# One Hydra mixer on one core: x times silu(z) formed ahead of the fd bank, and four orders of work rewritten

## The chip, the core and the metric

One core of one Trainium2 chip runs the whole program. The metric is the device time of one execution in microseconds. The profile is one execution, recorded by the hardware profiler; its times count from the first instruction. PE is TensorE, DVE is VectorE, ACT is ScalarE, POOL is GpSimd, SP is SyncE, which issues the DMAs.

## The reference

Two transformer-like blocks with AdaLN modulation over 1024 tokens of 512 features. Block 0 is attention and a routed MLP, block 1 a Hydra mixer and a gated MLP with LoRA. The change is in block 1's mixer, of which the kernel computes this part twice (y = 0, 1) for each half (hf) of 512 tokens:

```python
h = gelu(x @ w_down.T + b_down)
z, xBC = split(h @ in_w.T)
xs = silu(conv(xBC))                                  # sequence length 1: one tap
y  = xs * repeat(xs @ fcD_w.T + D, 64, axis=-1)       # the scans are shifted out at length 1
yz = y * silu(z)
h  = (yz * rsqrt(mean(yz ** 2) + 1e-5) * norm_w) @ out_w.T
# after the second pass:
h  = xmid + alpha * xmid + (1 - alpha) * h
x  = x_init + (h @ w_up.T + b_up)                     # then layernorm, modulation, MLP
```

## The kernel before

Features lie on the 128 partitions, tokens along the free axis, in two halves `tok[0]` and `tok[1]`. A half of a 256-feature tensor is two tiles (m = 0, 1) of 128x512 float32. TensorE writes into eight PSUM banks that are handed out in turn by a planner (`Banks`), whose order is that of the list `MIXER`; `filled` waits until TensorE has filled a bank, `evacuated` until its reader is done.

Each engine runs the mixer by a list of its own, written out by hand: `MIXER` (TensorE), `MIXER_ACT`, `MIXER_DVE`, `MIXER_POOL`. An engine works strictly in the order of its list. An entry is (step, y, hf):

- `mid`, `in`, `fd`: TensorE projects down, makes the xs and z banks (four matmuls), and from xs the two fd banks (four matmuls). ScalarE turns the first into xs and sz = silu(z).
- VectorE's `fd`, for each m: yz = (bank + D) * xs (line 2028), then yz = yz * sz (line 2032). `fd_first` and `fd_second` are m = 0 and m = 1.
- `out`: TensorE multiplies yz by Who (two matmuls) and sums squares, which ScalarE makes from yz (16 small matmuls); ScalarE copies the result to hor and the mean square to hms; GpSimd takes the inverse root (line 2364).
- `dg`: VectorE spreads the root into a diagonal tile (line 2041), both inputs in SBUF. `scale`: TensorE broadcasts it into the bank rbc (one matmul), VectorE multiplies it by hor into hof (2048, or 2053 for y = 1, there followed by 2055, which adds midf). hof feeds `in` of the next y, or `up`.
- `up`: TensorE makes two banks of 128x512; VectorE adds them to x (line 1894) and takes layernorm statistics (1652, 1658 to 1664) of what it has added.
- Beside this chain: `rows` prepares row vectors; `centred` (2001, eight tiles in all) writes rt; GpSimd's `shift` (2342) adds a row to x; `rest` (2007) adds rt times the deviation to x and must be done before `up`; `merge` (1996) adds LoRA to the next weights, ScalarE's and GpSimd's `w13` (1530, 2347) split them in two.

Behind the mixer GpSimd's root gives the last layernorm's scale, ScalarE normalises tiles 0 and 1 and VectorE tiles 2 and 3 (2074), TensorE transposes them (884), and VectorE, ScalarE and GpSimd split the transposed halves for the MLP (1691, 1695, 1355, 2174).

A step by VectorE or GpSimd that TensorE needs is signalled by a semaphore; SP's queue waits for freed weight slots (`piece_done`) and for `r_ready` before its next loads.

Of the kernel before, what the change touches and what calls it, by code (L numbers as in the profile page):

```python
# [23 lines left out]
ALU = mybir.AluOpType  # L24
# [7 lines left out]
KC = D // P  # L32
# [52 lines left out]
class Banks:  # L85
# [27 lines left out]
    def get(self, name, turn=0):  # L113
# [4 lines left out]

MIXER = [("mid", 0, 0), ("in", 0, 0), ("fd", 0, 0), ("ln", 0, 1), ("mid", 0, 1), ("out", 0, 0), ("in", 0, 1),
         ("scale", 0, 0), ("fd", 0, 1), ("in", 1, 0), ("out", 0, 1), ("fd", 1, 0), ("scale", 0, 1), ("in", 1, 1),  # L120
         ("lora", 0, 0), ("out", 1, 0), ("fd", 1, 1), ("scale", 1, 0), ("out", 1, 1), ("up", 0, 0), ("scale", 1, 1),
         ("up", 0, 1), ("up", 1, 0), ("up", 1, 1)]
MIXER_ACT = [("mid", 0, 0), ("in", 0, 0), ("ln", 0, 1), ("fd", 0, 0), ("mid", 0, 1), ("out", 0, 0), ("in", 0, 1),
             ("fd", 0, 1), ("in", 1, 0), ("out", 0, 1), ("fd", 1, 0), ("in", 1, 1), ("out", 1, 0), ("w13", 0, 0),
             ("fd", 1, 1), ("out", 1, 1)]
MIXER_DVE = [("fd", 0, 0), ("rows", 0, 0), ("dg", 0, 0), ("scale", 0, 0), ("fd", 0, 1), ("centred", 0, 0),
             ("centred", 0, 1), ("dg", 0, 1), ("fd_first", 1, 0), ("scale", 0, 1), ("fd_second", 1, 0), ("rest", 0, 0), ("merge", 0, 0),
             ("rest", 0, 1), ("dg", 1, 0), ("fd", 1, 1), ("scale", 1, 0), ("dg", 1, 1), ("up", 0, 0), ("scale", 1, 1),
             ("up", 0, 1), ("up", 1, 0), ("up", 1, 1)]
MIXER_POOL = [("out", 0, 0), ("wup", 0, 0), ("out", 0, 1), ("shift", 0, 0), ("shift", 0, 1), ("out", 1, 0),  # L130
              ("out", 1, 1), ("w13", 1, 1)]
FD_PARTS = {"fd": (0, 1), "fd_first": (0,), "fd_second": (1,)}
SPLIT_LNS = (1, 3)

# [263 lines left out]
def adaln_two_blocks(nc, a, out):  # L398
    banks, pieces, prods = plan()
    with ExitStack() as ctx:  # L400
# [12 lines left out]
        def sem(name):  # L413
            return ctx.enter_context(nc.semaphore(name))
# [4 lines left out]
        def ar(word, *dims):  # L419
# [183 lines left out]
        ab_in, ab_ready, rn_ready, xb_ready, r_ready = (  # L603
            sem("mixer_rows_loaded"), sem("mixer_rows_ready"), sem("mixer_rest_centred"),
            sem("mixer_rest_shifted"), sem("mixer_rest_ready"))
        yz_ready, sq_ready, ho_ready = sem("yz_ready"), sem("yz_squared"), sem("hydra_out_ready")
        eps_ready, hor_ready = sem("eps_ready"), sem("hydra_out_copied")
        ms_ready, mr_ready, dg_ready = sem("mean_squares_ready"), sem("inverse_rms_ready"), sem("inverse_rms_diagonal_ready")
# [1035 lines left out]
        def _(dve):  # L1644
            V = nc.vector
# [364 lines left out]
            for kind, y, hf in MIXER_DVE:  # L2010
# [11 lines left out]
                elif kind in FD_PARTS:  # L2022
                    for m in FD_PARTS[kind]:
                        n = 4 * y + 2 * hf + m
                        b = filled(dve, ("fd", y, hf, m))
                        if y:
                            dve.wait_ge(sq_ready, n - 3)
                        V.scalar_tensor_tensor(out=yz[:, m, tok[hf]], in0=ps[:, b, :], scalar=cols[:, C_D + m:C_D + m + 1],
                                               in1=xs[:, m, tok[hf]], op0=ALU.add, op1=ALU.mult).then_inc(read_b[b], 1)
                        evacuated(dve, ("z", y, hf, m))  # L2030
                        evacuated(dve, ("fd", y, hf, m))
                        V.tensor_tensor(yz[:, m, tok[hf]], yz[:, m, tok[hf]], sz[:, m, tok[hf]], ALU.mult)\
                            .then_inc(yz_ready, 1)
                elif kind == "rest":
                    for t in range(4 * hf, 4 * hf + 4):
                        rest(t)
# [20 lines left out]
                elif kind == "merge":  # L2057
                    for c in range(2):
                        merge(("w13", c), [("lora", "F", c), ("lora3", "F", c)])
                elif kind == "up":  # L2060
                    for t in (4 * y + 2 * hf, 4 * y + 2 * hf + 1):
                        add_x(("wup", t), t, x[:, t, :])
                        if t % 4:
                            evacuated(dve, ("wup", t - 1))
                            ln_stat(y, t % 4 - 1)
                    if hf:
                        evacuated(dve, ("wup", t))
                        ln_stat(y, 3)
                        ln_finish(3, y)
                    if (y, hf) == (1, 0):  # L2070
                        dve.wait_ge(ln_nb, 1)
                        filled(dve, ("ln", 2, 1, KC - 1))
                        for t in range(2, 4):
                            V.tensor_scalar(xnb[:, t, :], x[:, t, :], rs[:, 0, t:t + 1], nb[:, 0, t:t + 1], ALU.mult,
                                            ALU.add).then_inc(ln_xn, 1)
            ln_full(3, 0)
            ln_full(3, 1)

# [49 lines left out]
        def _(pool):  # L2128
# [230 lines left out]
            for kind, y, hf in MIXER_POOL:  # L2359
# [3 lines left out]
                        pool.wait_ge(dg_ready, 2 * y + hf)  # L2363
                    nc.gpsimd.tensor_tensor(hrs[:, :], hms[:, :], mh[:, :], ALU.pow).then_inc(mr_ready, 1)
                elif kind == "shift":
                    pool.wait_ge(dg_ready, 2)
                    for t in range(4 * hf, 4 * hf + 4):
                        rest(t)
                elif kind == "wup":
                    raw_loaded(pool, "wup")  # L2370
                    pool.wait_ge(rows_ready, 1)
                    nc.gpsimd.tensor_tensor(Wuo[:, :], raw[:, piece_slot("wup"), 0:D], t36[:, :], ALU.mult)\
                        .then_inc(piece_done, 1)
                elif kind == "w13":
                    pool.wait_ge(yz_ready, 4 * y + 2 * hf + 2)
                    for k in range(2):
                        w13_lo(k, ("w13", k), k)
            rstd(3, 0)
# [115 lines left out]
```

## Time and profile before

| | |
|---|---|
| median of 3 runs | 757.67 us (755.9 to 758.73) |
| span of the profiled execution | 756.9 us |
| TensorE matmul busy | 713.5 us, 94% |
| VectorE busy | 474.8 us, 63% |
| ScalarE busy | 318.3 us, 42% |
| GpSimd busy | 314.5 us, 42% |
| the mixer on TensorE | 482.64 to 556.28 us |

The profile names each instruction by engine, line, operation and tiles (output, arrow, inputs). A matmul of float32 is recorded as two instructions, so x8 are four matmuls. The square bracket at the end of a line is the time that the engine sat idle ahead of it and what ended that. A timeline row merges like neighbours: its start, and the time from the first start to the last end.

### The profile page before, as it was taken

Reading aid. Unit: us, or ns where it says so; the run is one execution under the profiler, and the core shown is the slowest. Engines: PE = TensorE matmul, PEld = TensorE weight load, DVE = VectorE, ACT = ScalarE, POOL = GpSimd, SP = SyncE. Lnnn points to the kernel's source line nnn. Section 1 sums busy time; section 2 is a strip of 40 time slices with the busy share of each in tenths; the row PEclk is TensorE's granted clock in tenths of the full one; section 3 lists DMA queues with packets and bytes.
Section 4 is the critical chain, followed back from the end, with each engine's and each line's share of the span. In section 5 each row is a group of like instructions: output and inputs, shape, how many; then the busy total and the mean of one; then the engine's idle time right before and its main releaser. Section 6 shows DMA issues by size and latency. Waiting matters only on the chain.

```text
span 756.9 us, 10266 instructions
## 1 busy us (share of the span) xinstructions
PE 713.5 (94%) x3718; PEld 431.1 (57%) x3718; DVE 474.8 (63%) x716; ACT 318.3 (42%) x536; POOL 314.5 (42%) x254
## 2 busy tenths in 40 slices
PE   4998899999999999889999999999789999999998
PEld 2444334333333332258788888554358788877886
DVE  3787677888888885237765558768895433338211
ACT  3311267677767767751335310554234223223100
POOL 0325673756565574861456233115431222125300
PEclk9999799999999999999999999999889999999999
DMA  8357516263251200230023100213010111111111
GB/s 307 107 126 220 124 43 164 73 123 54 72 123 26 30 3 29 75 113 14 29 62 105 56 1 0 78 50 66 1 68 1 57 55 39 44 55 57 42 69 42
DMA packets 24111, 53.00 MB, mean 70 GB/s; under 512 B 4252, under 2 KB 8100, under 8 KB 23044
## 3 DMA queue, kind: packets, MB, share of 16 engines
q1 hardware_dynamic: 24068, 52.44, 25.0%
q8 instruction: 26, 0.43, 0.2%
q14 instruction: 17, 0.14, 0.1%
HBM read 45.63 MB, written 6.60 MB: 69 GB/s over the span
## 4 chain that ended last, share of the span: by engine, by line
PE 76%; DVE 12%; issue 5%; DMA 2%; ACT 2%; SPq 2%; POOL 1%; DVEq 0%; ACTq 0%; POOLq 0%
PE ps L867 73%; DVE mxp L1810 2%; DMA rq<-in_mask 1%; DVE st L1652 1%; PE ps L884 1%; DVE xnb L1676 1%; ACT pr L1456 1%; DVE x L2007 1%; PE ps L1051 1%; DVE rt L1691 1%; DVE x L1894 1%; PE ps L1119 0%; DVE dg L2041 0%; SPq L717 0%; DVE qsw L1861 0%
## 5 line engine op out<-in xcount | busy, mean ns | idle before, releaser
L867 PE MATMUL ps<-arena 128*128 128x512 f32 (+1 forms) x1404 | 325.9, 392 | 1.4 <-DVE arena L1695 0.7
L867 PEld LDWEIGHTS ps<-arena 128*128 128x128 f32 (+1 forms) x1404 | 259.6, 186 | 59.3 <-DVE arena L1695 1.4
L1810 DVE TENSOR_REDUCE mxp<-ps 128x2 f32<-128x1024 f32 (+3 forms) x160 | 172.8, 1115 | 44.5 <-PE ps L867 43.9
L1456 ACT ACTIVATE pr<-ps 128x512 f32<-128x512 f32 x288 | 162.1, 596 | 75.7 <-PE ps L867 71.9
L867 PE MATMUL ps<-Qst,Kst 99*128 99x512 bf16 x288 | 100.2, 389 | 6.1 <-ACT pr L1456 4.8
L867 PE MATMUL ps<-Kst,Qst 96*128 96x512 bf16 (+3 forms) x384 | 98.6, 334 | 5.4 <-DVE mxp L1810 4.2
L2248 POOL TENSOR_TENSOR pr<-pr,cap 128x512 int32<-128x512 int32 x56 | 71.1, 1285 | 38.3 <-ACT pr L1456 38.3
L867 PE MATMUL ps<-pr,vr 128*32 128x512 f32 x576 | 76.5, 604 | 0.0
L867 PEld LDWEIGHTS ps<-Qst,Kst 99*128 99x128 bf16 x288 | 24.5, 98 | 79.7 <-ACT pr L1456 63.9
L867 PEld LDWEIGHTS ps<-Kst,Qst 96*128 96x128 bf16 x384 | 36.4, 99 | 51.3 <-DVE mxp L1810 20.2
L2347 POOL TENSOR_TENSOR arena<-raw,arena 128x1024 fp32r<-128x1024 f32 x11 | 26.7, 2431 | 80.2 <-ACT arena L1530 80.2
L867 PE MATMUL ps<-maskb,identb 128*128 128x128 bf16 (+1 forms) x264 | 53.1, 229 | 0.0
L2088 DVE TENSOR_TENSOR xnb<-ps,full 128x512 f32<-128x512 f32 x22 | 15.2, 691 | 49.0 <-PE ps L867 46.0
L1894 DVE TENSOR_TENSOR x<-ps,x 128x512 f32<-128x512 f32 x24 | 16.2, 685 | 46.2 <-PE ps L867 46.2
L1605 ACT ACTIVATE arena<-xnb 128x512 f32 (+1 forms) x22 | 13.9, 632 | 45.9 <-DVE xnb L2088 45.9
L2164 POOL TENSOR_TENSOR rs<-ve,mh 128x4 f32<-128x4 f32 x8 | 8.1, 1016 | 57.2 <-DVE ve L1664 57.1
L867 PEld LDWEIGHTS ps<-maskb,identb 128*128 128x128 bf16 x264 | 26.3, 100 | 8.5 <-issue 2.9
L867 PE MATMUL ps<-h0T,wq 128*128 128x512 f32 x64 | 30.0, 600 | 0.5 <-ACT wq L1389 0.5
L2090 DVE TENSOR_TENSOR arena<-xnb,arena 128x512 f32 (+1 forms) x22 | 15.3, 697 | 20.0 <-ACT arena L1605 20.0
L867 PEld LDWEIGHTS ps<-pr,vr 128*32 128x32 f32 x576 | 11.5, 108 | 24.0 <-issue 21.4
L1519 ACT ACTIVATE full<-ps,s 128x512 f32<-128x512 f32 x8 | 5.5, 689 | 45.9 <-PE ps L867 45.9
L2238 POOL TENSOR_TENSOR wsum<-wsum,wmr 128x640 f32<-128x640 f32 (+2 forms) x18 | 23.7, 1315 | 1.5
(203 smaller groups left out, 822.2 us busy)
## 6 DMA issues: line engine op xcount, KB each, us to landing
wmr<-in_wmr SPq DMA_DIRECT2D x8, 1280.0 KB, 11.0
raw<-in_w SPq DMA_DIRECT2D x16, 512.0 KB, 3.3
Qst<-q_parts SPq DMA_DIRECT2D x42, 128.0 KB
q_parts<-qparts SPq DMA_DIRECT2D x3, 768.0 KB, 5.0
x<-in_x SPq DMA_DIRECT2D x8, 256.0 KB, 6.0
wm<-in_wm SPq DMA_DIRECT2D x4, 512.0 KB, 7.5
raw<-in_up SPq DMA_DIRECT2D x8, 256.0 KB, 2.6
raw<-in_down SPq DMA_DIRECT2D x8, 256.0 KB, 2.6
```

What stands on the lines that cost most here:

```text
L867: return nc.tensor.matmul(outp, lhs, rhs, start=start, stop=stop, skip_group_check=True)
L884: last = nc.tensor.transpose(ps[:, b, t * P:(t + 1) * P], xnb[:, t, c * P:(c + 1) * P], ident[:, :])
L1456: A(pr[:, k % PRING, :], ps[:, 4 + k % 2, :], ACT.Exp, scale=float(DH) ** -0.5).then_inc(exp_done, 1)
L1605: A(gT[0][:, bass.ds(c, 1), tok[hf]].rearrange("p o n -> p (o n)"), xnb[:, s, :], ACT.Copy)\
L1810: V.tensor_reduce(mxp[:, kh, g0:g0 + heads, i].rearrange("p (b e) -> p b e", e=per), units, AXX, ALU.max)\
L1894: V.tensor_tensor(x[:, t, :], ps[:, b, :], other, ALU.add).then_inc(read_b[b], 1)
L2088: V.tensor_tensor(xnb[:, s, :], ps[:, b, :], full[:, s, :], ALU.mult).then_inc(read_b[b], 1)
L2090: V.tensor_tensor(gT[1][:, bass.ds(c, 1), tok[hf]].rearrange("p o n -> p (o n)"), xnb[:, s, :], gT[0][:, bass.ds(c, 1), tok[hf]].rearrange ...
L2164: root = nc.gpsimd.tensor_tensor(rs[:, hf, :], ve[:, hf, :], mh[:, :], ALU.pow)
L2238: ins = nc.gpsimd.tensor_tensor(wsum[:, n0:n1], wsum[:, n0:n1], to, ALU.add)
L2248: nc.gpsimd.tensor_tensor(v, v, cap[:, :].unsqueeze(1).to_broadcast([P, G, P]), ALU.mult).then_inc(masked, 1)
L2347: nc.gpsimd.tensor_tensor(W13[slot][1].rearrange("p a b c -> p (a b c)"), raw[:, piece_slot(name), :], W13[slot][0].rearrange("p a b c -> ...
```

## The change

VectorE gets a step `gate` that forms yz = xs * sz as soon as both are there, and its fd step becomes one pass, yz = (bank + D) * yz, after which it frees the bank. A new semaphore `xz_ready` goes between the two. The tiles 2 and 3 of the last normalisation become a step of their own, `norm`. The lists are rewritten: TensorE's `up(0,1)` goes ahead of `scale(1,1)`; VectorE's and GpSimd's lists as shown; GpSimd's shifts of half hf now wait for the diagonal of that half, and its `w13` waits for a diagonal in place of yz and stands ahead of the last root.

```diff
--- before.py
+++ after.py
@@ -118,17 +118,18 @@
 
 MIXER = [("mid", 0, 0), ("in", 0, 0), ("fd", 0, 0), ("ln", 0, 1), ("mid", 0, 1), ("out", 0, 0), ("in", 0, 1),
          ("scale", 0, 0), ("fd", 0, 1), ("in", 1, 0), ("out", 0, 1), ("fd", 1, 0), ("scale", 0, 1), ("in", 1, 1),
-         ("lora", 0, 0), ("out", 1, 0), ("fd", 1, 1), ("scale", 1, 0), ("out", 1, 1), ("up", 0, 0), ("scale", 1, 1),
-         ("up", 0, 1), ("up", 1, 0), ("up", 1, 1)]
+         ("lora", 0, 0), ("out", 1, 0), ("fd", 1, 1), ("scale", 1, 0), ("out", 1, 1), ("up", 0, 0), ("up", 0, 1),
+         ("scale", 1, 1), ("up", 1, 0), ("up", 1, 1)]
 MIXER_ACT = [("mid", 0, 0), ("in", 0, 0), ("ln", 0, 1), ("fd", 0, 0), ("mid", 0, 1), ("out", 0, 0), ("in", 0, 1),
              ("fd", 0, 1), ("in", 1, 0), ("out", 0, 1), ("fd", 1, 0), ("in", 1, 1), ("out", 1, 0), ("w13", 0, 0),
              ("fd", 1, 1), ("out", 1, 1)]
-MIXER_DVE = [("fd", 0, 0), ("rows", 0, 0), ("dg", 0, 0), ("scale", 0, 0), ("fd", 0, 1), ("centred", 0, 0),
-             ("centred", 0, 1), ("dg", 0, 1), ("fd_first", 1, 0), ("scale", 0, 1), ("fd_second", 1, 0), ("rest", 0, 0), ("merge", 0, 0),
-             ("rest", 0, 1), ("dg", 1, 0), ("fd", 1, 1), ("scale", 1, 0), ("dg", 1, 1), ("up", 0, 0), ("scale", 1, 1),
-             ("up", 0, 1), ("up", 1, 0), ("up", 1, 1)]
-MIXER_POOL = [("out", 0, 0), ("wup", 0, 0), ("out", 0, 1), ("shift", 0, 0), ("shift", 0, 1), ("out", 1, 0),
-              ("out", 1, 1), ("w13", 1, 1)]
+MIXER_DVE = [("gate", 0, 0), ("fd", 0, 0), ("rows", 0, 0), ("centred", 0, 0), ("dg", 0, 0), ("scale", 0, 0),
+             ("gate", 0, 1), ("fd", 0, 1), ("centred", 0, 1), ("rest", 0, 0), ("gate", 1, 0), ("dg", 0, 1),
+             ("fd_first", 1, 0), ("scale", 0, 1), ("fd_second", 1, 0), ("rest", 0, 1), ("merge", 0, 0),
+             ("gate", 1, 1), ("dg", 1, 0), ("fd", 1, 1), ("scale", 1, 0), ("up", 0, 0), ("dg", 1, 1),
+             ("up", 0, 1), ("scale", 1, 1), ("norm", 0, 0), ("up", 1, 0), ("up", 1, 1)]
+MIXER_POOL = [("out", 0, 0), ("wup", 0, 0), ("shift", 0, 0), ("out", 0, 1), ("shift", 0, 1), ("out", 1, 0),
+              ("w13", 1, 0), ("out", 1, 1)]
 FD_PARTS = {"fd": (0, 1), "fd_first": (0,), "fd_second": (1,)}
 SPLIT_LNS = (1, 3)
 
@@ -603,6 +604,7 @@
         ab_in, ab_ready, rn_ready, xb_ready, r_ready = (
             sem("mixer_rows_loaded"), sem("mixer_rows_ready"), sem("mixer_rest_centred"),
             sem("mixer_rest_shifted"), sem("mixer_rest_ready"))
+        xz_ready = sem("xs_times_gate_ready")
         yz_ready, sq_ready, ho_ready = sem("yz_ready"), sem("yz_squared"), sem("hydra_out_ready")
         eps_ready, hor_ready = sem("eps_ready"), sem("hydra_out_copied")
         ms_ready, mr_ready, dg_ready = sem("mean_squares_ready"), sem("inverse_rms_ready"), sem("inverse_rms_diagonal_ready")
@@ -2023,14 +2025,22 @@
                     for m in FD_PARTS[kind]:
                         n = 4 * y + 2 * hf + m
                         b = filled(dve, ("fd", y, hf, m))
+                        dve.wait_ge(xz_ready, n + 1)
+                        V.scalar_tensor_tensor(out=yz[:, m, tok[hf]], in0=ps[:, b, :], scalar=cols[:, C_D + m:C_D + m + 1],
+                                               in1=yz[:, m, tok[hf]], op0=ALU.add, op1=ALU.mult).then_inc(yz_ready, 1)
+                        dve.wait_ge(yz_ready, n + 1)
+                        nc.vector.sem_inc(read_b[b], 1)
+                elif kind == "gate":
+
+                    if y:
+                        filled(dve, ("hout", 0, hf))
+                    for m in range(2):
+                        evacuated(dve, ("xs", y, hf, m))
+                        evacuated(dve, ("z", y, hf, m))
                         if y:
-                            dve.wait_ge(sq_ready, n - 3)
-                        V.scalar_tensor_tensor(out=yz[:, m, tok[hf]], in0=ps[:, b, :], scalar=cols[:, C_D + m:C_D + m + 1],
-                                               in1=xs[:, m, tok[hf]], op0=ALU.add, op1=ALU.mult).then_inc(read_b[b], 1)
-                        evacuated(dve, ("z", y, hf, m))
-                        evacuated(dve, ("fd", y, hf, m))
-                        V.tensor_tensor(yz[:, m, tok[hf]], yz[:, m, tok[hf]], sz[:, m, tok[hf]], ALU.mult)\
-                            .then_inc(yz_ready, 1)
+                            dve.wait_ge(sq_ready, 2 * hf + m + 1)
+                        V.tensor_tensor(yz[:, m, tok[hf]], xs[:, m, tok[hf]], sz[:, m, tok[hf]], ALU.mult)\
+                            .then_inc(xz_ready, 1)
                 elif kind == "rest":
                     for t in range(4 * hf, 4 * hf + 4):
                         rest(t)
@@ -2067,12 +2077,12 @@
                         evacuated(dve, ("wup", t))
                         ln_stat(y, 3)
                         ln_finish(3, y)
-                    if (y, hf) == (1, 0):
-                        dve.wait_ge(ln_nb, 1)
-                        filled(dve, ("ln", 2, 1, KC - 1))
-                        for t in range(2, 4):
-                            V.tensor_scalar(xnb[:, t, :], x[:, t, :], rs[:, 0, t:t + 1], nb[:, 0, t:t + 1], ALU.mult,
-                                            ALU.add).then_inc(ln_xn, 1)
+                elif kind == "norm":
+                    dve.wait_ge(ln_nb, 1)
+                    filled(dve, ("ln", 2, 1, KC - 1))
+                    for t in range(2, 4):
+                        V.tensor_scalar(xnb[:, t, :], x[:, t, :], rs[:, 0, t:t + 1], nb[:, 0, t:t + 1], ALU.mult,
+                                        ALU.add).then_inc(ln_xn, 1)
             ln_full(3, 0)
             ln_full(3, 1)
 
@@ -2363,7 +2373,7 @@
                         pool.wait_ge(dg_ready, 2 * y + hf)
                     nc.gpsimd.tensor_tensor(hrs[:, :], hms[:, :], mh[:, :], ALU.pow).then_inc(mr_ready, 1)
                 elif kind == "shift":
-                    pool.wait_ge(dg_ready, 2)
+                    pool.wait_ge(dg_ready, hf + 1)
                     for t in range(4 * hf, 4 * hf + 4):
                         rest(t)
                 elif kind == "wup":
@@ -2372,7 +2382,7 @@
                     nc.gpsimd.tensor_tensor(Wuo[:, :], raw[:, piece_slot("wup"), 0:D], t36[:, :], ALU.mult)\
                         .then_inc(piece_done, 1)
                 elif kind == "w13":
-                    pool.wait_ge(yz_ready, 4 * y + 2 * hf + 2)
+                    pool.wait_ge(dg_ready, 2 * y + hf + 1)
                     for k in range(2):
                         w13_lo(k, ("w13", k), k)
             rstd(3, 0)
```

## Rows read from the trace of the kernel before

**Rows 1.** The page: busy time, share of span and instructions of each engine

```profile
PE 713.5 (94%) x3718; PEld 431.1 (57%) x3718; DVE 474.8 (63%) x716; ACT 318.3 (42%) x536; POOL 314.5 (42%) x254
```

**Rows 2.** TensorE's timeline through the mixer: start, us, line, operation, tiles

```profile
511.36 3.60 PE L867 MATMUL ps<-hof,Whi 128*128 128x512 f32 x8
514.79 1.88 PE L867 MATMUL ps<-yz,Who 128*128 128x512 f32 x4
...
521.73 1.02 PE L867 MATMUL ps<-dg,ones 128*128 128x512 f32 x2
523.60 3.70 PE L867 MATMUL ps<-hof,Whi 128*128 128x512 f32 x8 [0.85 <-DVE hof L2048]
...
531.51 3.68 PE L867 MATMUL ps<-xs,Wfd 128*128 128x512 f32 x8
537.73 1.75 PE L867 MATMUL ps<-dg,ones 128*128 128x512 f32 x2 [2.54 <-DVE dg L2041]
...
543.88 1.96 PE L867 MATMUL ps<-Wuo,hof 128*128 128x512 f32 x4
548.32 2.08 PE L867 MATMUL ps<-dg,ones 128*128 128x512 f32 x2 [2.48 <-DVE dg L2041]
550.18 6.10 PE L867 MATMUL ps<-Wuo,hof 128*128 128x512 f32 x12
558.90 3.45 PE L884 MATMUL ps<-ident,xnb 128*128 128x128 f32 x16 [2.62 <-ACT xnb L1592]
...
566.91 2.02 PE L867 MATMUL ps<-arena 128*128 128x512 f32 x7 [0.66 <-DVE arena L1695]
```

**Rows 3.** Table by stretches: busy time of each engine, granted clock, DMA

```profile
537.70:541.70 4.00, 3.97 (x5) 1.42 (x6) 3.76 (x6) 1.26 (x2) 0.00 (x0) 0.57 0.00 0
...
548.30:552.00 3.70, 3.68 (x5) 1.69 (x6) 3.21 (x5) 0.00 (x0) 2.17 (x1) 0.54 0.77 235
```

**Rows 4.** VectorE's timeline through the mixer

```profile
505.12 1.74 DVE L2041 TENSOR_TENSOR dg<-ident,hrs 128x512 f32<-128x512 f32 x1 [2.94 <-POOL hrs L2364]
...
513.02 5.38 DVE L2001 SCALAR_TENSOR_TENSOR rt<-x,mv,Abc 128x512 f32<-128x512 f32 x8
519.77 0.69 DVE L2041 TENSOR_TENSOR dg<-ident,hrs 128x512 f32<-128x512 f32 x1 [1.36 <-POOL hrs L2364]
...
531.95 2.47 DVE L1996 SCALAR_TENSOR_TENSOR raw<-ps,raw 128x512 f32<-128x512 f32 x4
534.35 2.72 DVE L2007 SCALAR_TENSOR_TENSOR x<-rt,rs,x 128x512 f32<-128x512 f32 x4
536.99 0.68 DVE L2041 TENSOR_TENSOR dg<-ident,hrs 128x512 f32<-128x512 f32 x1
...
545.44 2.82 DVE L2041 TENSOR_TENSOR dg<-ident,hrs 128x512 f32<-128x512 f32 x1 [3.46 <-POOL hrs L2364]
...
558.53 0.68 DVE L1894 TENSOR_TENSOR x<-ps,x 128x512 f32<-128x512 f32 x1
...
562.25 0.17 DVE L1664 TENSOR_SCALAR ve<-mv 128x4 f32<-128x4 f32 x1
562.33 2.97 DVE L1691 TENSOR_SCALAR rt<-ps,modc 128x512 f32<-128x512 f32 x4
```

**Rows 5.** GpSimd's timeline through the mixer

```profile
520.54 12.62 POOL L2342 TENSOR_TENSOR x<-x,Bbc 128x512 f32<-128x512 f32 x8 [0.81 <-DVE dg L2041]
...
544.39 1.01 POOL L2364 TENSOR_TENSOR hrs<-hms,mh 128x4 f32<-128x4 f32 x1 [10.27 <-ACT hms L1579]
545.37 5.10 POOL L2347 TENSOR_TENSOR arena<-raw,arena 128x1024 fp32r<-128x1024 f32 x2
```

**Rows 6.** Groups of VectorE's passes by line; last, durations of line 2007, min/median/max

```profile
L2032 DVE TENSOR_TENSOR yz<-yz,sz 128x512 f32<-128x512 f32 x8 | 6.0, 748 | 0.8
L2028 DVE SCALAR_TENSOR_TENSOR yz<-ps,cols,xs 128x512 f32<-128x512 f32 x8 | 6.0, 746 | 1.3 <-PE ps L867 1.1 <-DVE hof L2048 0.2
...
L2007 DVE SCALAR_TENSOR_TENSOR x<-rt,rs,x x8: 735/1244/1764, 525.2 to 536.3; 128x512 f32<-128x512 f32 x8
```

## The prediction

> **What bounds the kernel now.** I read the page's busy times first: TensorE is busy 94% of the span [rows 1], so the kernel can only gain where TensorE waits or runs slowly. TensorE's timeline through the mixer is next [rows 2]. Up to 535.2 us it hardly pauses: the largest hole, 0.85 us, is ahead of 523.60. Then three holes come in a row: 2.54 us ahead of 537.73, 2.48 us ahead of 548.32 and 2.62 us ahead of 558.90; a smaller one (0.66 us) ahead of 566.91. The granted clock falls from full (2.4 GHz) to half (1.2 GHz) behind each large hole [rows 3]: a float32 matmul of 128x512 takes 0.86 us at full clock (3.43 for the four from 511.36 to 514.79), so the seven from 548.32 to 556.28 should take 6.2 us with their tail and take 7.96, a loss of 1.8 us; the transposes at 558.90 take 3.45 us and should take about 2. Together: 8.3 us of holes and about 5 us of slow clock. Everything behind 567 us is TensorE's own work and moves with it.
>
> VectorE's timeline says why [rows 4]. Ahead of 537.73 TensorE wants the diagonal dg(1,0); VectorE begins it at 536.99, after the merges and four residual passes (rest) that end at 537.07, though GpSimd's root had come at 534.1 (behind eight shifts that end at 533.16 [rows 5]). Ahead of 548.32 it wants dg(1,1): its root is done at 545.40, but the pass takes 2.82 us instead of 0.68, because GpSimd starts its w13 subtraction at 545.37 [rows 5]. Ahead of 558.90 it wants normalised x, which needs VectorE's sums of up(0,1), queued behind scale(1,1).
>
> **Price of contention.** A VectorE pass whose two inputs are both in SBUF is stretched by a GpSimd pass: a rest takes 0.74 us alone and up to 1.76 beside the shifts (+1.03), dg +2.14 beside the longer w13 pass [rows 4 to 6]. The fd pass that reads PSUM takes 0.74 to 0.75 in all eight places, two of them during the shifts [rows 6]. So the new fd pass (PSUM and yz) is immune, and the new gate passes (xs, sz) are exposed: 0.69 each alone, 1.7 (a shift) to 2.8 (a w13 pass) blocked.
>
> The Trainium skill's page "SBUF — State Buffer", section "Who interferes with whom", says that a VectorE instruction with two SBUF inputs and a GpSimd instruction that reads SBUF exclude each other for the whole instruction. The trace agrees (0.68 against 2.82 us); it speaks against moving more two-input passes among the shifts, and feeds the last rival.
>
> **The change, part by part.**
>
> 1. *Gate formed early.* Per half, four passes (0.74 + 0.69, twice) behind the fd bank become two (0.74 each) behind it and two gates before. VectorE's sum stays: 2.9 us. Behind the second bank's fill the path shrinks from 1.55 to 0.75 us. For halves (0,0), (0,1), (1,0) TensorE asks for yz later than it was ready even before, so that is worth nothing; it counts in (1,1).
>
> 2. *Half (0,1) and the first shifts.* centred(0,0) (4 x 0.67 = 2.7 us) goes into the 2.94 us in which VectorE idled before dg at 505.12 [rows 4]: free. shift(0,0) now starts when dg(0,0) is done, 506.9, and runs beside gate(0,1), which starts about 508.9 (506.9, TensorE's broadcast 1.3, the hof pass 0.7). With two blockings the gates end at 512.1, the fd passes at 513.7, before out(0,1) at 514.79: hidden with 1.1 us over. Then VectorE has centred(0,1) 2.7, rest(0,0) 2.7 and gate(1,0) 1.4: it reaches dg(0,1) at 520.4, not 519.77. TensorE needs that dg at 521.73 [rows 2], so 0.6 us of cover is left and 523.60 stays. Bounds: nothing, to 2.5 us late (four shift passes can block four passes, 4.1 us; two are in my value, and 0.6 is covered, so 1.5, plus a blocking of up to 1.0 by the 1.01 us root).
>
> 3. *Half (1,0) into (1,1), the first large hole.* VectorE is free at 524.5. shift(0,1) has begun at about 521.0 and ends near 527; rest(0,1) is done near 528.9 (two blocked), merges 2.47 us to 531.4, gate(1,1) to 532.8. GpSimd's root no longer waits for shifts: its input comes 0.5 us behind the issue of TensorE's next step (543.88 and 544.39 [rows 2, 5]; here 531.51), at 532.0, root 533.0, dg(1,0) to 533.7. TensorE's fd(1,1) issues until 534.95, so the hole is gone. fd(1,1)'s last pass runs 535.1 to 535.8, and out(1,1) issues at 535.8. The w13 subtractions now wait for dg(1,0), 533.7 to 538.8, and beside them scale(1,0)'s second pass (midf and hof, both in SBUF, due at 536.7) is blocked by up to 2.1 us: 539.4 against 539.2 when TensorE wants it. up(0,0) starts at about 539.45 instead of 543.88: **4.4 us** gained, 2.5 of hole, the rest clock. Bounds: if every rest is blocked (4 x 1.7) and both gates, dg(1,0) ends near 536.6: the gain shrinks to 1.1.
>
> 4. *Half (1,1), the second hole.* The root comes 0.5 us behind up(0,0)'s issue as before [rows 2, 5], ending at 540.75 with GpSimd free from 538.8. But dg(1,1) is now queued on VectorE behind up(0,0): add, add, sums. The second bank fills at 541.3, so these end at 542.5 and dg(1,1) at 543.2, without the 2.1 us of contention. up(0,1) covers TensorE until 542.9: a hole of 0.3 us. scale(1,1) issues at 543.2 and fills at 544.2. On VectorE it now stands behind up(0,1), whose two adds, three statistics and small passes take 3.9 us (the same set runs from 558.53 to 562.42 [rows 4]): 543.1 to 547.0, then hof's two passes to 548.4. Only then can up(1,0) go. So 2.48 us of hole become **4.2 us** at another place, and the clock falls there again (1.8 us lost on the four matmuls): up(1,1) fills at 553.8 against 556.4. Of 4.4 us, 1.8 are given back here. Bounds: 1.4 to 3.5 us lost to the clock.
>
> 5. *Third hole.* up(0,1)'s statistics are done at 547.0, the root at 548.3, ScalarE's and VectorE's normalised tiles by 550.0: before up(1,1) ends, so the transposes follow it at once at 553.8 (558.90 before) at full clock. "norm" standing ahead of up(1,0) on VectorE costs nothing: it ends at 549.4 and the first bank fills at 550.3. What is late next is VectorE's tail: up(1,1)'s set starts at 553.25 (bank and queue), 3.9 us, then 4.45 us from 562.42 to the release at about 566.87 [rows 2, 4]: 553.25 + 3.9 + 4.45 = 561.6. TensorE waits there about 1.4 us where it waited 0.66.
>
> **Sum.** 566.9 − 561.6 = 5.3 us. Cross-check by holes and clock: 8.3 + 5.3 before; 0.3 + 4.2 + about 2.0 (of it 0.6 on ScalarE's halves) + 1.8 after, which is 5.3 less. The profiled execution spans 756.9 us and the median of the runs is 757.67, 0.7 above it; 756.9 − 5.3 = 751.6 for a span, **752.4** for a median. Loads for w13 start when slots are freed, now about 9 us earlier; the swap of up(0,1) and scale(1,1) only exchanges banks that are read long before.
>
> **Rivals.**
> - *Better cover.* The clock does not fall behind the 4.2 us hole, or is full again by the time matmuls resume: 1.8 less, 750.6. Against it: each of three holes above 2.4 us was followed by half clock [rows 2, 3]. Chance 0.10.
> - *Given back.* The clock falls also behind the last wait (1.4 us, between the 0.85 that left it full and the 2.48 that did not), 1.7 us, and dg(1,0) or the hof combine comes up to 1.5 us late: 754.1 to 755.9, taken as 755. Chance 0.24.
> - *It does not do what it says.* VectorE's queue is still at rest and merge at 535 to 536, so dg(1,0) moves by 1 us only, and the long hole of part 4 eats that: 757. For it: VectorE's queue has no pause from 531.95 to 537.67 [rows 4]. Against: four rests (2.7 us) left that stretch. Chance 0.06.
> - *Slower: two-input passes blocked in series.* From the moment merge ends after about 533.8, ScalarE's w13 copies run to 536, the w13 subtractions to 541, and VectorE's hof combine and dg stand in them: 2.1 us twice. With 1.5 us lost in part 2, 3.3 in part 3 (4.4 to 1.1), and the clock lost at the end (1.7): 752.4 + 4.2 + 1.5 + 3.3 + 1.7 = 763 at worst; three quarters of it, 760, is taken. It decides once 5.3 us of it, half, fall in the path. The rule quoted above from the Trainium skill's page "SBUF — State Buffer" is the same mechanism. Chance 0.08.
>
> **How the numbers follow.** Forecast 0.52 (751 to 753.9). This kernel's measurement can tell about 0.5% (3.8 us) from no change, so faster means below 753.9: 0.52 + 0.10 + 0.02 of the given-back case = 0.64. Same: 0.22 + 0.06 = 0.28. Slower: 0.08. Range 749.6 to 756.8: it takes in the better case and its own spread, the given-back case, and leaves out about 0.04 below and 0.12 above.
>
> **What would show it.** Right: TensorE without a hole before scale(1,0); dg(1,1) at 0.7 us; a hole of about 4 us before up(1,0), with half clock behind it; transposes directly behind up(1,1). Wrong: gate(0,1) or rest blocked so often that TensorE waits ahead of in(1,1) or scale(1,0) by over 1 us; dg above 1 us; half clock after TensorE's wait for VectorE's halves.

## The result and the profile after

The changed kernel takes 753.56 us (median of 7 runs, 751.74 to 754.48) beside 756.89 for the kernel before in the same runs. The ratio is 0.9944, with a 95% interval of 0.9928 to 0.996: by the ratio 4.2 us faster (0.56%), by the two medians 3.3. The forecast was 752.4, the range 749.6 to 756.8.

The profiled execution of the changed kernel took 754.48 us and spans 752.7; before it spanned 756.9. TensorE is busy for 1.8 us less, as the page's first row shows (engines, busy us, share of the span), which answers to [rows 1]:

```profile
PE 711.7 (95%) x3718; PEld 429.2 (57%) x3718; DVE 472.8 (63%) x716; ACT 318.0 (42%) x536; POOL 314.6 (42%) x254
```

So of the 4.2 us some 2.4 are waiting, and 1.8 are the same 3718 matmul records in less time: over the mixer stretch that is measured below, the granted clock averages 0.91 of full before and 0.94 after. TensorE's timeline of the changed kernel, beside [rows 2]:

```profile
507.89 3.60 PE L869 MATMUL ps<-xs,Wfd 128*128 128x512 f32 x8
...
523.67 3.70 PE L869 MATMUL ps<-hof,Whi 128*128 128x512 f32 x8 [0.86 <-DVE hof L2058]
...
531.58 3.68 PE L869 MATMUL ps<-xs,Wfd 128*128 128x512 f32 x8
535.10 1.02 PE L869 MATMUL ps<-dg,ones 128*128 128x512 f32 x2
...
539.58 3.67 PE L869 MATMUL ps<-Wuo,hof 128*128 128x512 f32 x8
543.51 1.12 PE L869 MATMUL ps<-dg,ones 128*128 128x512 f32 x2 [0.26 <-DVE dg L2051]
548.78 6.54 PE L869 MATMUL ps<-Wuo,hof 128*128 128x512 f32 x8 [4.14 <-issue]
555.16 1.91 PE L886 MATMUL ps<-ident,xnb 128*128 128x128 f32 x16
...
562.63 2.03 PE L869 MATMUL ps<-arena 128*128 128x512 f32 x7 [1.16 <-DVE arena L1697]
```

The hole of 2.54 us ahead of scale(1,0) is gone (535.10 follows fd(1,1) at once), and up(0,0) starts at 539.58 instead of 543.88. The hole ahead of scale(1,1) is 0.26 us instead of 2.48. A new one of 4.14 us stands ahead of up(1,0), at 548.78; its bracket says `issue`, which names no releaser, and VectorE's second pass into hof, which up(1,0) reads, ends just before, at 548.68. The four matmuls behind it, eight records, take 6.54 us; at full clock the four of up(0,0) and up(0,1) take 3.67. The transposes follow without a hole. The last wait is 1.16 us instead of 0.66. The clock column of the table by stretches (seventh figure behind the times, as in [rows 3]) shows the half clock behind the new hole:

```profile
544.60:548.80 4.20, 0.06 (x2) 0.05 (x1) 3.97 (x13) 0.03 (x1) 1.32 (x2) 0.87 0.00 0
548.80:555.20 6.40, 6.40 (x9) 2.62 (x10) 3.88 (x7) 1.49 (x2) 0.00 (x0) 0.55 0.00 0
```

VectorE's timeline, beside [rows 4]: the two gates of half (0,1) among the shifts, dg(0,1), the combine of scale(1,0), dg(1,1), and the two hof passes of scale(1,1).

```profile
509.09 2.58 DVE L2042 TENSOR_TENSOR yz<-xs,sz 128x512 f32<-128x512 f32 x2 [0.23 <-DVE hof L2058]
...
520.95 0.69 DVE L2051 TENSOR_TENSOR dg<-ident,hrs 128x512 f32<-128x512 f32 x1 [0.91 <-POOL hrs L2374]
...
537.02 2.46 DVE L2065 SCALAR_TENSOR_TENSOR hof<-midf,alf,hof 128x512 f32<-128x512 f32 x1
...
542.78 0.68 DVE L2051 TENSOR_TENSOR dg<-ident,hrs 128x512 f32<-128x512 f32 x1
...
547.20 0.69 DVE L2063 TENSOR_TENSOR hof<-ps,hor 128x512 f32<-128x512 f32 x1
547.93 0.75 DVE L2065 SCALAR_TENSOR_TENSOR hof<-midf,alf,hof 128x512 f32<-128x512 f32 x1
```

dg(1,1) takes 0.68 us, not 2.82. The combine, 0.75 us alone, takes 2.46 beside the w13 subtractions, and the two gates 2.58, not 1.28. GpSimd's timeline, beside [rows 5]: the root of half (0,1), and the two w13 subtractions.

```profile
518.70 2.22 POOL L2374 TENSOR_TENSOR hrs<-hms,mh 128x4 f32<-128x4 f32 x1 [5.90 <-ACT hms L1581]
...
534.26 4.67 POOL L2357 TENSOR_TENSOR arena<-raw,arena 128x1024 fp32r<-128x1024 f32 x2 [0.81 <-DVE dg L2051]
```

The root takes 2.22 us instead of 1.01: gate(1,0) runs on VectorE meanwhile. dg(0,1) ends at 521.64, and TensorE's scale(0,1) issues at 521.69, so the cover of 0.6 us that the prediction counted had shrunk to nothing.

**A measure for the experiments.** Whole times scatter by about 0.5% for one kernel, so each profile is also read over one stretch: from the first matmul of fd(0,1) to the release of the first MLP wait (the start of the x7 group). The kernel before begins its stretch with this row:

```profile
507.92 3.60 PE L867 MATMUL ps<-xs,Wfd 128*128 128x512 f32 x8
```

It is 566.91 − 507.92 = **58.99 us** before and 562.63 − 507.89 = **54.74 us** after, 4.25 us less: the whole difference of the spans (4.2) lies in it. What comes behind the stretch takes 190.0 to 190.1 us in every profile but e9's; what comes ahead of it varies by up to 6 us (503.51 in e6 to 509.44 in e5), though no edit touches it.

A stretch is one execution. The same kernel gave 54.74 and 54.22 us (e11), and the difference comes from the clock behind the new hole: up(1,0) starts 40.89 and 40.90 us into it. So for differences below 0.5 us I read where up(1,0) starts. The ratios, of 4 to 10 runs each, don't bear out every size. Put over the span of 756.9 us, the stretches of e1 (0.990), e4 (0.991), e3 and e6 (1.002) and e7 (1.003) lie outside the intervals of their own whole times in the table. What an edit does to the order of work is read from the stretch; how much it gives on average is not.

### The profile page after: what moved, and what is told of

The parts are those of the page before. It is cut to its first block, busy times and chain, and to the rows that moved or that the text cites. A ratio compares the mean times of both kernels' runs of the same rounds, so it can differ in the third digit from the quotient of the medians.

```text
span 752.7 us, 10280 instructions
## 1 busy us (share of the span) xinstructions
PE 711.7 (95%) x3718; PEld 429.2 (57%) x3718; DVE 472.8 (63%) x716; ACT 318.0 (42%) x536; POOL 314.6 (42%) x254
## 4 chain that ended last, share of the span: by engine, by line
PE 79%; DVE 10%; issue 4%; DMA 2%; ACT 2%; SPq 2%; POOL 1%; DVEq 0%; ACTq 0%; POOLq 0%
PE ps L869 76%; DVE mxp L1812 2%; DMA rq<-in_mask 1%; PE ps L886 1%; DVE st L1654 1%; DVE xnb L1678 1%; ACT pr L1458 1%; PE ps L1053 1%; DVE rt L1693 1%; PE ps L1121 0%; SPq L719 0%; DVE x L1896 0%; DVE qsw L1863 0%; DMA q_parts<-parts 0%; POOL arena L2357 0%
## 5 line engine op out<-in xcount | busy, mean ns | idle before, releaser
L1896 DVE TENSOR_TENSOR x<-ps,x 128x512 f32<-128x512 f32 x24 | 16.4, 687 | 50.2 <-PE ps L869 50.2
L2343 POOL TENSOR_TENSOR yrs<-yve,mh 128x1 f32<-128x1 f32 x8 | 6.0, 755 | 43.9 <-DVE yve L1974 43.9
```

The source lines that it names most:

```text
L1896: V.tensor_tensor(x[:, t, :], ps[:, b, :], other, ALU.add).then_inc(read_b[b], 1)
```

## The experiments

| kernel | stretch, us | ratio to before (95%) |
|---|---|---|
| before | 58.99 | |
| changed | 54.74 | 0.9944 (0.9928 to 0.996) |
| e11, changed again | 54.22 | 0.9934 (0.991 to 0.9957) |
| e1, tail as before | 51.68 | 0.993 (0.9906 to 0.9953) |
| e2, w13 behind the root | 55.06 | 0.9949 (0.9929 to 0.9969) |
| e3, no gate | 60.67 | 1.0 (0.9981 to 1.0018) |
| e4, hole filled | 52.39 | 0.9943 (0.992 to 0.9965) |
| e5, no gate, w13 behind | 55.17 | 0.9956 (0.9942 to 0.997) |
| e6, shifts as before | 60.16 | 0.9988 (0.9973 to 1.0003) |
| e7, gate alone on before | 61.30 | 0.9988 (0.9972 to 1.0004) |
| e8, e1 with norm on ScalarE | 53.04 | 0.9906 (0.9882 to 0.993) |
| e9, VectorE's tail alone | 53.27 | 0.9931 (0.9914 to 0.9949) |
| e10, e1 with its hole filled | 51.86 | 0.992 (0.9894 to 0.9945) |

**1. Which order took the first hole away.** e6 keeps gate, w13 and tail, and puts the residual work back on both engines (... stands for what is left out):

```diff
-             ... ("centred", 0, 0), ("dg", 0, 0), ..., ("centred", 0, 1), ("rest", 0, 0), ("gate", 1, 0), ("dg", 0, 1), ...,
-             ("rest", 0, 1), ("merge", 0, 0), ("gate", 1, 1), ("dg", 1, 0), ...
+             ... ("dg", 0, 0), ..., ("centred", 0, 0), ("centred", 0, 1), ("gate", 1, 0), ("dg", 0, 1), ...,
+             ("rest", 0, 0), ("merge", 0, 0), ("rest", 0, 1), ("gate", 1, 1), ("dg", 1, 0), ...
-             ... ("wup", 0, 0), ("shift", 0, 0), ("out", 0, 1), ("shift", 0, 1), ...      # MIXER_POOL
+             ... ("wup", 0, 0), ("out", 0, 1), ("shift", 0, 0), ("shift", 0, 1), ...
-                    pool.wait_ge(dg_ready, hf + 1)      # each shift
+                    pool.wait_ge(dg_ready, 2)
```

> The changed kernel, gates, w13 and tail included, with centred, rest and merge on VectorE and the shifts on GpSimd in the order of the kernel before, both shifts behind the second diagonal. Theory (the early shifts and rests made the hole ahead of scale(1,0) go): dg(1,0) runs at about 538 on the clock of the kernel before, a hole of 3 to 4 us and half clock are back; same stretch 59 to 61 us, 4 to 6 more than the changed kernel. Rival (another part removed that hole): within 1 us of 54.74.

The stretch is 60.16 us, 5.4 more than in the changed kernel. TensorE's timeline of e6, scale(1,0) and up(0,0), has the hole again, and behind it a wait of 0.83 us. The row names w13, but that had ended at 538.43; the combine on VectorE, the last row here, takes 2.71 us beside w13 (late too now) and ends at 538.97:

```profile
533.72 1.13 PE L869 MATMUL ps<-dg,ones 128*128 128x512 f32 x2 [2.95 <-DVE dg L2051]
...
539.07 5.20 PE L869 MATMUL ps<-Wuo,hof 128*128 128x512 f32 x8 [0.83 <-POOL arena L2357]
```

```profile
536.26 2.71 DVE L2065 SCALAR_TENSOR_TENSOR hof<-midf,alf,hof 128x512 f32<-128x512 f32 x1
```

The theory holds, and the size is as forecast. The whole times agree: the interval of e6 (0.9973 to 1.0003) lies above that of the changed kernel. Moving the residual work forward is what makes the first hole go; VectorE's order and GpSimd's were moved back together, so their shares aren't known.

**2. What the gate is worth.** e7 puts it alone into the kernel before, e3 takes it out of the changed one, e5 takes it out and moves w13 back too, e2 moves only w13 back. e3 and e5 pass over the step `gate` and use the fd step of the kernel before:

```diff
-  V.scalar_tensor_tensor(out=yz[...], in0=ps[:, b, :], ..., in1=yz[...], ...)
+  V.scalar_tensor_tensor(out=yz[...], in0=ps[:, b, :], ..., in1=xs[...], ...)
+  V.tensor_tensor(yz[...], yz[...], sz[...], ALU.mult)
```

e2 and e5 change GpSimd's list:

```diff
-              ("w13", 1, 0), ("out", 1, 1)]
+              ("out", 1, 1), ("w13", 1, 1)]
-                    pool.wait_ge(dg_ready, 2 * y + hf + 1)
+                    pool.wait_ge(yz_ready, 4 * y + 2 * hf + 2)
```

> The changed kernel's orders with the fd step of the kernel before: no gate, two passes behind each bank. Theory (the orders make the gain, the gate takes next to nothing off the path): out(1,1)'s second matmul waits about 0.2 us, the hof pass ahead of in(1,1) starts 0.1 to 0.3 us later; 0.2 to 0.6 us more than the changed kernel, ratio to before about 0.995. Rival (the gate carries the gain, 0.8 us at each half that is on the path): 1.6 to 3 us more, ratio 0.996 to 0.998.

> The changed kernel with GpSimd's two w13 subtractions back behind the last root, waiting for yz as before. Theory (the move is worth what dg(1,1) lost to contention, 2.1 us, less what the hof combine of (1,0) loses now): the combine takes 0.75 us instead of 2.46, up(0,0) starts 0.2 us earlier, dg(1,1), now at 542.78, falls into the subtractions (540.9 to 546) and takes 1.1 to 2.8 us; 0.3 to 2 us more than the changed kernel, ratio to before 0.995 to 0.997. Rival (with dg queued behind up(0,0), the move no longer matters): within 0.3 us of the changed kernel.

> The kernel without the gate (e3_two_pass_fd) and with GpSimd's w13 subtractions back behind the last root. Read from fd(0,1)'s first matmul to the release of the first MLP wait, which took 58.99 us before, 54.74 in the changed kernel and 60.67 without the gate. Theory (the gate's worth is only that no two-input pass of fd(1,1) meets the w13 subtractions): the passes of fd(1,1) take 0.7 each again, the loss of 5.9 us goes almost wholly, 55.3 us. Rival (the longer chain behind the fd bank costs by itself): 57 us or more.

> The kernel before with the gate and one-pass fd alone; all other steps in the order of the kernel before. Theory (alone it saves 0.8 us behind the last fd bank at best, where TensorE waits for dg and not for yz): stretch 58.0 to 59.5 us, ratio 0.998 to 1.001. Rival (the gate's own worth is the larger part of the gain): 56 us or less.

e3 refuted my theory, and its rival was too mild: the stretch is 60.67 us, 5.9 more, and the whole gain is gone (ratio 1.0, interval above that of the changed kernel). VectorE's timeline of e3 shows the second passes of fd(1,1), 0.69 us alone:

```profile
531.76 2.21 DVE L2034 TENSOR_TENSOR yz<-yz,sz 128x512 f32<-128x512 f32 x1
...
534.74 1.99 DVE L2034 TENSOR_TENSOR yz<-yz,sz 128x512 f32<-128x512 f32 x1
```

Both inputs are in SBUF, and both run beside the w13 subtractions (531.07 to 536.18), GpSimd's row:

```profile
531.07 5.11 POOL L2360 TENSOR_TENSOR arena<-raw,arena 128x1024 fp32r<-128x1024 f32 x2 [0.80 <-DVE dg L2054]
```

TensorE's timeline of e3, the two matmuls of out(1,1):

```profile
534.11 1.10 PE L869 MATMUL ps<-yz,Who 128*128 128x512 f32 x2 [0.84 <-DVE yz L2034]
536.78 2.07 PE L869 MATMUL ps<-yz,Who 128*128 128x512 f32 x2 [1.57 <-DVE yz L2034]
```

They wait 0.84 and 1.57 us, and the clock then drops. With w13 moved back as well (e5) the passes take 0.69 each and the stretch is 55.17 us: 0.1 more than e2 (55.06), which has the gate. TensorE's up(1,0) with (1,1), first of e2, then of e5:

```profile
548.33 6.52 PE L869 MATMUL ps<-Wuo,hof 128*128 128x512 f32 x8 [4.15 <-issue]
```

```profile
550.73 6.66 PE L869 MATMUL ps<-Wuo,hof 128*128 128x512 f32 x8 [4.14 <-issue]
```

Counted from the stretch's start (507.13 and 509.44) they begin at 41.20 and 41.29 us, so the 0.1 us is there ahead of the clock too. The long chain costs next to nothing by itself; 5.5 of the 5.9 us that e3 loses are the collision. VectorE's timeline of e2, the combine and dg(1,1):

```profile
536.25 0.75 DVE L2065 SCALAR_TENSOR_TENSOR hof<-midf,alf,hof 128x512 f32<-128x512 f32 x1
...
541.82 1.19 DVE L2051 TENSOR_TENSOR dg<-ident,hrs 128x512 f32<-128x512 f32 x1
```

The combine is clean (0.75 for 2.46), dg is stretched by half a microsecond (1.19 for 0.68), and the balance is 0.32 us, the bottom of the range that the theory gave and the top of the rival's: the two can't be told apart. dg(1,1), queued behind up(0,0), meets only the end of the first subtraction. Gate and early w13 together are thus worth 55.17 − 54.74 = 0.4 us in these profiles (41.29 − 40.89 at up(1,0)). The ratios (0.9944, 0.9949, 0.9956) can't tell the three kernels apart.

e7's time is that of the kernel before within its interval, which the theory said, but its stretch is 61.30, outside. TensorE's timeline of e7, scale(1,0), out(1,1) and up(0,0):

```profile
534.01 1.13 PE L868 MATMUL ps<-dg,ones 128*128 128x512 f32 x2 [1.74 <-DVE dg L2050]
535.96 3.75 PE L868 MATMUL ps<-yz,Who 128*128 128x512 f32 x4 [0.83 <-DVE yz L2028]
...
542.78 3.76 PE L868 MATMUL ps<-Wuo,hof 128*128 128x512 f32 x4
```

The hole is shorter (1.74 us), yet the second wait behind it (0.83) and a half clock that lasts from 535 to 552 us lose more than that. The gate of (1,1) stands between dg(1,0) and fd(1,1) there, where it hides nothing and is itself what out(1,1) waits for. The size isn't typical: this execution's mean clock, 0.984, is the lowest of the ten (the others 0.989 to 0.995), and their ratio (0.9972 to 1.0004) has no room for 2.3 us more. That the gate alone brings nothing, both show.

**3. The new hole.** e1 puts the end of both lists back:

```diff
 MIXER:     - ("up", 0, 0), ("up", 0, 1), ("scale", 1, 1), ("up", 1, 0)
            + ("up", 0, 0), ("scale", 1, 1), ("up", 0, 1), ("up", 1, 0)
 MIXER_DVE: - ("up", 0, 0), ("dg", 1, 1), ("up", 0, 1), ("scale", 1, 1), ("norm", 0, 0), ("up", 1, 0), ("up", 1, 1)
            + ("dg", 1, 1), ("up", 0, 0), ("scale", 1, 1), ("up", 0, 1), ("up", 1, 0), ("norm", 0, 0), ("up", 1, 1)
```

> The changed kernel with the end of TensorE's and VectorE's lists in the order of the kernel before: scale(1,1) ahead of up(0,1) on TensorE; on VectorE dg(1,1) ahead of up(0,0), scale(1,1) ahead of up(0,1), norm behind up(1,0). Theory (the new tail costs: dg and scale(1,1) wait in VectorE's queue behind up, which opens the 4.14 us hole): root at 540.9, dg to 541.6, scale(1,1) on VectorE behind up(0,0) to about 544.8, up(1,0) on TensorE at about 545 instead of 548.78 with hardly a hole; a hole of about 3 us comes back ahead of the transposes, at about 551.5 instead of 555.16; the first MLP wait ends near 559.2 instead of 562.63: 3.4 us less than the changed kernel, ratio to before about 0.990. Rival (the new tail pays, since it removes the hole ahead of the transposes): 2 us more than the changed kernel, ratio about 0.997.

Its TensorE timeline, from scale(1,1) to the first MLP wait:

```profile
538.52 1.12 PE L869 MATMUL ps<-dg,ones 128*128 128x512 f32 x2 [0.15 <-DVE dg L2051]
...
541.74 3.67 PE L869 MATMUL ps<-Wuo,hof 128*128 128x512 f32 x8 [0.38 <-issue]
548.42 2.66 PE L886 MATMUL ps<-ident,xnb 128*128 128x128 f32 x16 [3.01 <-ACT xnb L1594]
...
556.42 2.03 PE L869 MATMUL ps<-arena 128*128 128x512 f32 x7 [0.52 <-DVE arena L1697]
```

up(1,0) has 0.38 us of hole instead of 4.14 and starts 37.0 us into the stretch instead of 40.9. A hole of 3.01 us is back ahead of the transposes, and still the stretch is 51.68 us, 3.06 less than in the changed kernel (3.4 forecast). The ratio doesn't tell the two apart (0.993, from 4 runs). e9 changes VectorE's order alone, from up(0,1) on:

```diff
-             ("up", 0, 1), ("scale", 1, 1), ("norm", 0, 0), ("up", 1, 0), ("up", 1, 1)]
+             ("scale", 1, 1), ("up", 0, 1), ("up", 1, 0), ("norm", 0, 0), ("up", 1, 1)]
```

> The changed kernel with only VectorE's last steps in another order: scale(1,1) ahead of up(0,1), norm behind up(1,0); TensorE's order and dg(1,1) behind up(0,0) stay. The stretch is again from fd(0,1)'s first matmul to the release of the first MLP wait (54.74 us in the changed kernel, 51.68 in e1_tail_as_before). Theory (of the hole of 4.14 us, the larger part is scale(1,1) standing behind up(0,1) on VectorE): the hole shrinks to 1.5 us, the clock stays full, VectorE's last statistics end 2.2 us earlier, stretch 52.5 us. Rival (dg(1,1) behind up(0,0) and TensorE's swap are what costs): 54 us or more.

```profile
543.35 3.67 PE L869 MATMUL ps<-Wuo,hof 128*128 128x512 f32 x8 [1.68 <-issue]
550.03 1.97 PE L886 MATMUL ps<-ident,xnb 128*128 128x128 f32 x16 [3.01 <-ACT xnb L1594]
```

(TensorE's timeline of e9, up(1,0) with (1,1), and the transposes.) The hole is 1.68 us, and 1.5 of the 3.06 us are gained: between theory and rival. The other 1.6 go with dg(1,1) behind up(0,0) and TensorE's own swap, together; which of the two wasn't tried.

In this profile the 1.5 us are lost again behind the stretch, where 191.6 us follow and not 190.0. The MLP's first matmuls and the next transposes, behind the last wait, run partly at half clock, as the timeline and the table by stretches show:

```profile
558.00 2.65 PE L869 MATMUL ps<-arena 128*128 128x512 f32 x7 [1.28 <-DVE arena L1697]
560.45 2.96 PE L886 MATMUL ps<-ident,xnb 128*128 128x128 f32 x16
```

```profile
560.00:562.00 2.00, 2.00 (x10) 1.77 (x9) 0.00 (x0) 0.46 (x1) 0.00 (x0) 0.50 0.00 0
```

The same groups take 2.03 and 1.91 us in the changed kernel. And here the hole of 3.01 us left the clock full (1.97 us for the transposes), where the one of e1 did not (2.66).

**4. The clock behind the hole.** e4 puts matmuls into it, and leaves all orders alone:

```diff
+  if (y, hf) == (1, 0):
+      b = bank_of(pe, ("wup", 4))
+      for _ in range(4):
+          mm(ps[:, b, :], hof[:, tl(0)], Wuo[:, :], True, True)
   pe.wait_ge(ho_ready, 2 + y + 1)
```

> The changed kernel with four extra matmuls, whose result is overwritten, on TensorE ahead of up(1,0), in the hole of 4.14 us. Theory (my term for the clock was too small: 6.83 us at half clock, 3.1 us lost instead of 1.8): the extra matmuls run from about 544.5 to 547.9 at full clock, the clock stays full, up(1,0) and (1,1) take 3.6 us instead of 6.54; VectorE then has no pause, its last statistics end at about 555.4 instead of 558.2: 2.8 us less than the changed kernel, ratio to before about 0.9907. Rival (VectorE's queue sets this stretch at any clock): within 0.5 us of the changed kernel.

TensorE's timeline of e4, the extra matmuls, up(1,0) with (1,1), and the first MLP wait:

```profile
543.68 3.60 PE L869 MATMUL ps<-Wuo,hof 128*128 128x512 f32 x8
547.93 3.70 PE L869 MATMUL ps<-Wuo,hof 128*128 128x512 f32 x8 [0.66 <-DVE hof L2069]
...
559.49 2.03 PE L869 MATMUL ps<-arena 128*128 128x512 f32 x7 [1.28 <-DVE arena L1701]
```

The four real ones take 3.70 us, not 6.54, and the stretch is 52.39 us, 2.35 less (2.8 forecast); up(1,0) itself could go no earlier (40.83 us into the stretch, 40.89 in the changed kernel). So of what the new hole costs in that profile, 2.35 us is the clock, and TensorE did more work in less time. That filling the hole makes the kernel faster on average isn't shown: its ratio, from 4 runs, is 0.9943 beside 0.9944. e11 is the changed kernel once more:

> The changed kernel itself, beside e9_vector_tail_alone and e10_tail_filled on the same chip, and a second look at its clock. Theory (a hole above 4 us is followed by 6.8 us at half clock, as in four of the five profiles that had it, and not by 3.4): stretch 54.7 us, half clock for 6.8 us behind the hole. Rival (6.8 was chance): 3.4 us, stretch 53.5 us.

The stretch is 54.22 us. TensorE's timeline, then the table by stretches (granted clock seventh), for the same matmuls as in the changed kernel's row of 548.80 to 555.20:

```profile
545.47 5.78 PE L869 MATMUL ps<-Wuo,hof 128*128 128x512 f32 x8 [4.15 <-issue]
```

```profile
545.40:551.10 5.70, 5.63 (x9) 2.36 (x10) 3.53 (x7) 1.52 (x2) 0.03 (x1) 0.62 0.00 0
```

Here the half clock had begun earlier in the hole and ended earlier behind it: the four matmuls take 5.78 us instead of 6.54. The loss is 2.1 us in one execution and 2.9 in the other, and behind the same hole 1.7 in e3 (5.37 us) and 3.0 in e5 and e6 (6.66): not one figure. The rival's 3.4 us at half clock did not come here; its stretch of 53.5 did not either.

**5. What bounds the stretch then.** e8 takes VectorE's last normalising passes off it, e10 fills e1's hole:

```diff
 e8 (on e1):  - ("up", 1, 0), ("norm", 0, 0), ("up", 1, 1)]      + ("up", 1, 0), ("up", 1, 1)]
              - for t in range(4 if hf else 2):                  + for t in range(4):     # ScalarE
 e10 (on e1): + three matmuls, as in e4, ahead of ln_turn(3, 0)
```

> e1_tail_as_before with the normalisation of tiles 2 and 3 moved from VectorE to ScalarE, which stands idle there. Theory (in e1 VectorE is without a pause from 537.8 us to the first MLP wait and sets its end): the two passes' 0.99 us go, the transposes start later by up to 1.5 us, still in time; stretch 50.7 instead of e1's 51.68 us, about 0.987 of before. Rival (the transposes become late and TensorE's half clock eats it): 51.5 to 53 us.

> e1_tail_as_before with three extra matmuls, whose result is overwritten, in the hole of 3.01 us ahead of the transposes. Theory (there VectorE's queue sets the end, not the clock: it has no pause from 537.8 us on): the clock stays full, the first MLP matmuls end sooner and TensorE waits longer for VectorE, stretch 51.4 to 51.7 us, as e1. Rival (the half clock behind the hole sets the end): 50 us.

TensorE's timeline of e8, the transposes, and of e10, up(1,0) with the extra matmuls, the transposes and the first MLP wait:

```profile
552.11 3.67 PE L886 MATMUL ps<-ident,xnb 128*128 128x128 f32 x16 [4.42 <-ACT xnb L1594]
```

```profile
543.93 6.25 PE L869 MATMUL ps<-Wuo,hof 128*128 128x512 f32 x14 [0.38 <-issue]
550.61 1.97 PE L886 MATMUL ps<-ident,xnb 128*128 128x128 f32 x16 [0.44 <-ACT xnb L1597]
...
558.58 2.03 PE L869 MATMUL ps<-arena 128*128 128x512 f32 x7 [1.28 <-DVE arena L1700]
```

e8 goes the rival's way: its hole is 4.42 us, the transposes take 3.67 at half clock, and the stretch, read by the end of the same group (562.07 − 2.03 for its length), is 53.04 us, 1.4 more than e1. Its time (0.9906) can't be told from e1's. e10 keeps the clock full and gains nothing: 51.86 us against e1's 51.68, with the wait for VectorE grown from 0.52 to 1.28. In that order VectorE sets the end. Of the kernels timed, e1 and e10 have the shortest stretches; their intervals overlap those of the changed kernel (0.9944 and 0.9934), so that they are faster than it is what the profiles show, and not the whole times.

## Why the prediction was right

- **Part 1, the gate.** "Worth nothing" in three halves, and a path of 0.75 instead of 1.55 us in (1,1): right for the passes, and e5 against e2 prices the long chain at 0.1 us. What the prediction missed is that the early w13 of part 3 is only affordable because of the gate: without it the second passes and w13 collide, and the stretch is 5.9 us longer (e3).
- **Part 2, half (0,1).** The gates' end at 511.7 (512.1 said), the hole of 0.86 us kept: right, though the two gates took 2.58 us together, one full blocking and not the two that were counted. The cover at dg(0,1) was 0.05 us, not 0.6. The term missing is that gate(1,0) holds back GpSimd's small root, by 1.2 us; the prediction has only the opposite, up to 1.0 us by which the root would block a pass, and as a bound.
- **Part 3, the first hole.** dg(1,0) at 533.49 (533.0 said), no hole, the combine blocked to 539.5 (539.4), up(0,0) at 539.58 (539.45): right, 4.3 us of the 4.4 said, and e6 gives it back.
- **Part 4, the second hole.** A hole of 4.14 us (4.2 said) ahead of up(1,0): right. The term that was mis-sized is the clock behind it, taken from [rows 2] as 1.8 us, where holes were at most 2.62 us long. It was 2.9 us here and 2.1 in e11, inside the bounds of 1.4 to 3.5 that the prediction gave. That is most of the 1.1 us by which 5.3 us were too many. The cross-check that also came to 5.3 did so by luck: it has 5.3 us of slow clock before where the first paragraph has about 5, and TensorE's busy time in the stretch (49.84 us before, 48.25 after, of it 2.9 lost) makes it about 4.5.
- **Part 5, the third hole.** Transposes at once, at full clock, and a last wait of 1.16 us (1.4 said), for VectorE: right.
- **From span to median.** The prediction set 756.9 against 757.67 and added 0.7. The profiled execution of before had in fact taken 758.73 us, the slowest of its three, 1.8 over its span; the changed kernel's took 754.48 on a span of 752.7, 1.8 too. Like against like, the spans differ by 4.2 us, as the ratio has it, and the medians by 3.3. The forecast of 752.4 came within 1.2 us of 753.56 with some luck: it started from 757.67, and over seven runs the kernel before has 756.89, so that against the medians the gain of 5.3 us is 2.0 too many.
- **Rivals.** "Given back" was half true: the clock took more, but at the known hole, not at the last wait, behind which the clock stayed full; in e9, with a last wait of 1.28 us, it did fall. "Better cover" was held off with three holes that were each followed by half clock; e9's hole of 3.01 us, which was not, shows that three were few. The slower rival's mechanism is real, as e3 shows, but needed the second pass that the gate had removed.

The Trainium skill's rule on the shared interface ("SBUF — State Buffer", "Who interferes with whom") agrees with the stretched passes shown here: 2.46 and 1.99 to 2.21 us beside w13, where fd passes that read PSUM stay at 0.74 or 0.75. The Trainium skill's page "TensorE: Matmul & The Clock Gate", Part 1, says that activity releases the throttle. e4 is in line with it: busy through the hole, the four matmuls behind it took 3.70 us. e7 is not plainly so: its clock stayed at half for 17.1 us, of which TensorE was busy for 16.1.

## What to carry to other kernels

Ask of each reordering what it puts in front of the step that the bounding engine waits for next: here moving residual work ahead of the diagonals paid 5.4 us, and putting VectorE's sums in front of the last diagonal and scale pass, with TensorE's own swap, gave 3.1 back (both by single profiles; the whole times bear out the first alone). A pass with two SBUF inputs on VectorE's critical path and a long GpSimd pass must not be scheduled together; making the operand early took that pass off the path and let the GpSimd work move, provided that it is queued where VectorE would wait anyhow (in e7 it was not). A hole on TensorE costs its length and then the clock: price both, look at more than one profile for the second, and let the measured stretch reach past the last matmuls that the clock can still slow.

## What was not expected of the hardware

The block works both ways: GpSimd's root over 128x4 elements takes 1.01 us alone and 2.22 beside two gates.

The same kernel reaches the mixer at different times. fd(0,1) starts at 507.89 us in the changed kernel's profile and at 504.57 in e11's, and the difference begins far ahead of anything changed, in the table by stretches (granted clock seventh; the changed kernel, then e11):

```profile
80.00:100.00 20.00, 17.24 (x84) 6.82 (x82) 15.70 (x20) 7.73 (x15) 15.63 (x8) 0.74 0.56 147
```

```profile
80.00:100.00 20.00, 16.36 (x99) 6.20 (x99) 17.44 (x23) 9.56 (x17) 16.37 (x9) 1.00 0.50 137
```

One had half clock for part of 80 to 100 us, the other none, with TensorE busy for 17.2 and 16.4 of the 20 us. These 3.3 us at fd(0,1) are as large as the effect studied, which is why whole times alone could not rank the variants. What decides it was not found.
